# Loading adjacency chunks in transfers of 16 partitions instead of 8

## The chip, the cores and the metric

The kernel runs on one core of a Trainium2 chip. The metric is the device time of one execution in microseconds; lower is better. A separate execution is recorded by the hardware profiler, and all rows shown here come from that one.

## What is computed

Two graph layers over 4096 nodes with 128 features, each with a normalization ahead of it and a residual sum behind it. The adjacency is a 4096 x 4096 matrix of f32, 64 MiB, so reading it and keeping it in another order are the bulk of the traffic.

```python
h = relu(layernorm(x))
# layer 0
z = leaky_relu(lap_mul(adj, h) @ W1 + b1, 0.1)     # lap_mul(A, x) = d * (A @ (d * x)), d = 1/sqrt(row sums of A)
S = exp(-sqrt(pairwise squared distances of z) / 2), only the 4 largest of each row kept
x = x + lap_mul(S + adj, h) @ W2 + b2
# layer 1
h = relu(layernorm(x))
x = x + h @ W_self.T + (adj @ h) @ W_neigh.T + b
```

## The kernel before

The first stage reads the adjacency from HBM. A chunk is 2 MB: all 128 partitions, 16 rows of 256 columns each, so a partition gets 16 pieces of 1 KB that lie 64 matrix rows apart in HBM. There are eight groups g of four chunks c (`part_a`, in order of g and c), and then twelve chunks that are read a second time (`part_b`, groups from the last to the first): 44 chunks, 92.3 MB. They go into `araw`, which has four slots of one chunk; in `part_b` three of them are used.

GpSimd issues all loads (`load_first`, L367). Ahead of a chunk it waits until the chunk that was in the slot has been read (`chunk_read`). A chunk is split by `load_chunk`. The 128 partitions are four quarters q of R = 32; the transfers first take the quarters 0 and 2 in turn, then 1 and 3 in turn. SPREAD says how many transfers a quarter is split into and how far apart the partitions of one transfer are:

```python
def load_chunk(gp, g, c, place):
    for quarter_pair in ((0, 2), (1, 3)):
        for first in range(SPREAD):
            for q in quarter_pair:
                gp.dma_start(araw[R * q + first:R * q + R:SPREAD, place],
                             adj_v[q, first:R:SPREAD, g // 2, g % 2, :, c]).then_inc(a_first_in[place], DMA)
```

Whoever reads a chunk waits until the semaphore of its slot says that all of its transfers have landed (`PER_LOAD = QD * SPREAD * DMA`). ScalarE or VectorE sums its rows (`row_sums`, L618; L869), VectorE transposes it in blocks of 32 x 32 into units of 1 MB (`unit`, L840), and TensorE multiplies the units with the scaled features (`first_unit`, L1145). SyncE stores each of the 64 units to HBM (`transposed`, `keep_unit`, L408) for the later stages, while the loads go on. So in the first stage 92 MB are read on the queue of GpSimd, q0 in the trace, and 67 MB written on the queue of SyncE, q1; ScalarE's small stores of `hw_scratch` are on q10.

Behind it come the search for the four nearest nodes of each node (from about 500 us on), then two passes over the stored units. In them, GpSimd gathers rows with indirect transfers (L511, L587). Between the stages x is loaded once more (`xs`, 64 transfers of 32 partitions in 512 B pieces, each in one quarter, L428), and `hw_scratch` is loaded back by four transfers of 32 partitions, one for each quarter in turn (L447).

Of the kernel before, what the change touches and what calls it, by code (L numbers as in the profile page):

```python
# [42 lines left out]
SLOTS = 4  # L43
TSLOTS = 4
TOPK = 4
SPREAD = 4
LN_EPS = 1e-5
DMA = 16

# [1 line left out]
def gnn_kernel(nc, x, adj, W1, b1, W2, b2, W, b, out):  # L51
# [16 lines left out]
    with ctx:  # L68
# [251 lines left out]
        F1 = list(reversed(range(GROUPS)))  # L320
        PER_LOAD = QD * SPREAD * DMA
        X_IN = QD * GROUPS * DMA
# [40 lines left out]
# [7 lines that stand above are left out]
# [996 lines left out]
```

## Time and profile before

| | us |
|---|---|
| median of 3 runs (1219.0 to 1224.53) | 1224.19 |
| the profiled execution, its own time | 1223.94 |
| its span, first to last instruction | 1222.1 |
| TensorE busy | 969.5 |
| VectorE busy | 797.8 |
| GpSimd busy | 722.6 |
| ScalarE busy | 544.3 |

The span is a little shorter than the time of the execution. An engine's busy time counts its computing and, on GpSimd, the issuing of transfers; matrix multiplies overlap, so a busy TensorE isn't one at its peak. In the views of transfers, a queue's share is the time that its packets took, as a share of all 16 DMA engines over the stretch; since packets can overlap, a little over 100% can come out.

### The profile page before, as it was taken

What the parts mean: (1) busy time and instruction counts of PE and PEld (TensorE: products, weight loads), DVE (VectorE), ACT (ScalarE), POOL (GpSimd) and SP (SyncE); (2) the same over time, 40 slices, a digit from 0 to 9 for tenths busy, and PEclk for the clock granted to TensorE, in tenths of its full rate; (3) what the DMA queues carried; (4) which work ended last, traced back from release to release, by engine and by line L of the source; (5) the groups of instructions that cost most, each with busy time, mean ns of one, the idle gap of its engine ahead of it and who ended that gap; (6) DMA issues with size and microseconds to landing.
All of it is one profiled execution on the core that took longest, in us unless ns stands there. A gap on an engine that the chain in (4) does not pass through costs nothing.

```text
span 1222.1 us, 12797 instructions
## 1 busy us (share of the span) xinstructions
PE 969.5 (79%) x3506; PEld 649.9 (53%) x3506; DVE 797.8 (65%) x824; ACT 544.3 (45%) x1090; POOL 722.6 (59%) x1105
## 2 busy tenths in 40 slices
PE   0145635757868877899999996499999998999998
PEld 0122322323334333577777775266666666888886
DVE  1644644446357735399999999736666556788885
ACT  2455342644603211455555554523334334567663
POOL 9999999998839782144444444488778872000000
PEclk9977668878979989899999999699999999899999
DMA  9999999999999997685333336698888887699993
GB/s 219 322 313 329 316 336 358 350 364 350 376 349 369 367 366 281 189 271 214 139 141 141 142 143 225 196 365 329 312 309 303 305 327 273 244 385 392 363 392 110
DMA packets 126984, 353.67 MB, mean 289 GB/s; under 512 B 43232, under 2 KB 68576, under 8 KB 102368
## 3 DMA queue, kind: packets, MB, share of 16 engines
q1 hardware_dynamic: 55264, 243.75, 52.2%
q0 software_dynamic: 62464, 105.28, 29.3%
q10 hardware_dynamic: 9216, 4.20, 1.2%
q8 instruction: 14, 0.23, 0.1%
q14 instruction: 26, 0.21, 0.1%
HBM read 245.83 MB, written 106.95 MB: 289 GB/s over the span
## 4 chain that ended last, share of the span: by engine, by line
PE 31%; POOL 14%; issue 10%; DVE 6%; DMA 4%; ACT 2%; POOLq 0%; DVEq 0%; ACTq 0%; SPq 0%
POOL zt_lo L587 11%; PE ps L1255 5%; PE ps L1256 5%; PE ps L1257 5%; PE ps L1234 4%; PE ps L1237 4%; PE ps L1235 4%; PE ps L1236 4%; DMA araw<-in_adj_dram 3%; POOL araw L367 1%; POOL t_st L511 1%; DVE m L977 1%; PE ps L1145 1%; DVE i L979 1%; ACT araw L713 1%
## 5 line engine op out<-in xcount | busy, mean ns | idle before, releaser
L367 POOL DMA_DIRECT2D araw<-in_adj_dram x704 | 413.8, 597 | 44.1 <-DVE tr L840 28.3
L1089 DVE TENSOR_TENSOR araw_r<-araw,tr_r 128x2048 fp32r<-128x2048 f32 x96 | 217.5, 2289 | 89.6 <-ACT tr_r L740 89.5
L740 ACT ACTIVATE tr_r<-araw 128x2048 fp32r<-128x2048 f32 x96 | 181.4, 1910 | 81.2 <-DMA araw<-transposed 34.5
L587 POOL DMA_INDIRECT zt_lo<-neighbour_table,idx_st x128 | 175.9, 1374 | 46.0 <-issue 39.4
L713 ACT ACTIVATE araw<-ps,nsq 128x1024 f32<-128x1024 f32 x128 | 142.9, 1117 | 113.1 <-PE ps L1237 94.7
L1145 PE MATMUL ps<-tr,ys 128*128 128x512 f32 x256 | 131.8, 666 | 28.8 <-DVE ys L847 21.6
L618 ACT ACTIVATE ps<-araw 128x256 f32<-128x256 f32 x304 | 111.5, 367 | 84.0 <-DMA araw<-in_adj_dram 81.6
L1264 PE MATMUL ps<-araw,ys 128*128 128x512 f32 x256 | 117.0, 600 | 17.6 <-DVE ys L1012 17.6
L840 DVE STREAM_TRANSPOSE tr<-araw 128x2048 f32<-128x2048 f32 x32 | 72.8, 2295 | 67.7 <-DMA araw<-in_adj_dram 60.6
L869 DVE TENSOR_REDUCE part<-araw 128x16 f32<-128x4096 f32 x13 | 57.4, 4416 | 90.3 <-DMA araw<-in_adj_dram 62.0
L1234 PE MATMUL ps<-sq_rows,pick 128*128 128x512 f32 x256 | 102.2, 399 | 16.7 <-ACT araw L713 7.4
L1255 PE MATMUL ps<-araw_r,zt_hi 128*128 128x512 f32 x256 | 103.0, 402 | 4.9 <-DVE araw_r L1089 4.9
L1145 PEld LDWEIGHTS ps<-tr,ys 128*128 128x128 f32 x256 | 53.3, 216 | 93.8 <-issue 65.7
L1256 PE MATMUL ps<-tr_r,sq_rows 128*128 128x512 f32 x256 | 101.5, 396 | 0.0
L1257 PE MATMUL ps<-tr_r,zt_hi 128*128 128x512 f32 x256 | 101.2, 395 | 0.0
L1235 PE MATMUL ps<-zt_lo,zs_hi 128*128 128x512 f32 x256 | 100.5, 393 | 0.0
L1236 PE MATMUL ps<-zt_hi,zs_lo 128*128 128x512 f32 x256 | 100.4, 392 | 0.0
L1237 PE MATMUL ps<-zt_hi,zs_hi 128*128 128x512 f32 x256 | 100.4, 392 | 0.0
L511 POOL DMA_INDIRECT t_st<-keys_scratch,block_row x64 | 66.6, 1041 | 30.7 <-issue 25.1
L1264 PEld LDWEIGHTS ps<-araw,ys 128*128 128x128 f32 x256 | 48.7, 193 | 67.1 <-issue 65.1
L1171 PE MATMUL ps<-part,fold 128*128 128x16 f32 x64 | 14.1, 360 | 82.2 <-DVE part L869 82.2
L977 DVE MAX8 m<-araw 128x8 f32<-128x4096 f32 x16 | 70.9, 4430 | 9.7 <-ACT araw L713 9.3
(155 smaller groups left out, 1562.6 us busy)
## 6 DMA issues: line engine op xcount, KB each, us to landing
araw<-transposed SPq DMA_DIRECT2D x128, 1024.0 KB, 6.3
araw<-in_adj_dram POOLq DMA_DIRECT2D x704, 128.0 KB, 10.1
transposed<-tr SPq DMA_DIRECT2D x32, 1024.0 KB, 8.3
keys_scratch<-araw SPq DMA_DIRECT2D x64, 512.0 KB, 4.3
transposed<-unit_zt_hi SPq DMA_DIRECT2D x8, 1024.0 KB, 8.2
transposed<-unit_zt_lo SPq DMA_DIRECT2D x8, 1024.0 KB, 8.3
transposed<-unit_sq_rows SPq DMA_DIRECT2D x8, 1024.0 KB, 8.8
transposed<-araw SPq DMA_DIRECT2D x8, 1024.0 KB, 8.2
```

Of the source, the lines that this page charges most:

```text
L367: gp.dma_start(araw[R * q + first:R * q + R:SPREAD, place], adj_v[q, first:R:SPREAD, g // 2, g % 2, :, c]).then_inc(a_first_in[place], DMA)
L587: gp.indirect_dma_start(out=gath[:, i, u, k, :], out_offset=None, in_=table, in_offset=bass.IndirectOffsetOnAxis(ap=idx_st[:, i, u * TOPK ...
L713: act.activation(keys[par][:, c * 1024:c * 1024 + 1024], ps[:, 2 * c:2 * c + 2].rearrange("p a b -> p (a b)"), ACT.Identity, bias=nsq[:, b ...
L740: act.activation(ring_hi[:, place % TSLOTS], ring[:, j], ACT.Copy).then_inc(hi_done, 1)
L1089: v.tensor_tensor(ring_lo[:, j], ring[:, j], ring_hi[:, place % TSLOTS].bitcast(F32), ALU.subtract).then_inc(lo_done, 1)
L1145: pe.matmul(acc[bank], ys[:, i * GROUPS + j], rhs[:, i], start=start and i == 0, stop=stop and i == U - 1)\
L1234: pe.matmul(ps[:, c], pick[:], sq, start=True, stop=False)
L1235: pe.matmul(ps[:, c], zs_hi[:, par], zl, start=False, stop=False)
L1255: pe.matmul(acc[bank], hi[:, t], t_lo, start=j == 0 and i == 0, stop=False)
L1256: pe.matmul(acc[bank], lo[:, t], t_hi, start=False, stop=False)
L1257: ins = pe.matmul(acc[bank], hi[:, t], t_hi, start=False, stop=j == GROUPS - 1 and i == U - 1)
L1264: ins = pe.matmul(acc[bank], ys[:, i * GROUPS + j], ring[:, j, i], start=j == 0 and i == 0, stop=j == GROUPS - 1 and i == U - 1)
```

## The change

The number of transfers for a quarter goes from four to two, and with it the distance of the partitions of one transfer from four to two. A transfer then has 16 partitions instead of 8 and 256 KB instead of 128 KB, and a chunk is loaded by eight transfers instead of sixteen. The order of the quarters stays: 0, 2, 0, 2, 1, 3, 1, 3 now. The semaphore of a slot counts half as far, since `PER_LOAD` follows from the constant. Nothing else changes.

```diff
@@ -43,7 +43,7 @@
 SLOTS = 4
 TSLOTS = 4
 TOPK = 4
-SPREAD = 4
+SPREAD = 2
 LN_EPS = 1e-5
 DMA = 16
```

The instructions that GpSimd issues in the first stage, before (-) and now (+); a row gives the line, the operation, what it writes and reads, and its shape (partitions x pieces x elements) and number:

```order
@@ -8,5 +8,5 @@
 L484 AFFINE_SELECT ident<-ident 128x128
 L488 AFFINE_SELECT fold<-fold 128x128 x4
-L367 DMA araw<-in_adj_dram 8x16x256 x704
+L367 DMA araw<-in_adj_dram 16x16x256 x352
 L529 MEMSET sq_rows 64x4096
 L498 COPY zs_hi<-zt_hi 128x128
```

All other engines have the same instructions in the same order; on GpSimd the loads keep their place and there are half as many.

## Rows read from the trace of the kernel before

**Rows 1.** The page: span, then busy tenths in 40 equal slices.

```profile
span 1222.1 us, 12797 instructions
...
PE   0145635757868877899999996499999998999998
...
DVE  1644644446357735399999999736666556788885
ACT  2455342644603211455555554523334334567663
POOL 9999999998839782144444444488778872000000
...
DMA  9999999999999997685333336698888887699993
```

**Rows 2.** Transfers by queue from 0 to 485 us: packets, MB, share.

```profile
DMA packets 75095, 162.72 MB, mean 336 GB/s; under 512 B 35872, under 2 KB 44576, under 8 KB 67104
...
q0 software_dynamic: 56320, 92.68, 64.3%
q1 hardware_dynamic: 14144, 67.70, 35.2%
q10 hardware_dynamic: 4608, 2.10, 1.5%
```

**Rows 3.** Timeline of GpSimd: start, duration, instruction, count, idle before and releaser.

```profile
3.81 272.79 POOL L367 DMA_DIRECT2D araw<-in_adj_dram  x464 [0.37 <-POOL fold L488]
280.38 18.80 POOL L367 DMA_DIRECT2D araw<-in_adj_dram  x32 [3.79 <-ACTq L622]
```

**Rows 4.** Transfers from 77 to 86 us; an issue's last number is us to landing.

```profile
q0 software_dynamic: 1597, 2.63, 105.6%
...
araw<-in_adj_dram POOLq DMA_DIRECT2D x16, 128.0 KB, 4.5
```

**Rows 5.** The same from 270 to 300 us.

```profile
DMA packets 4339, 10.65 MB, mean 355 GB/s; under 512 B 2298, under 2 KB 2298, under 8 KB 3788
...
araw<-in_adj_dram POOLq DMA_DIRECT2D x44, 128.0 KB, 23.1
```

**Rows 6.** Waits from 0 to 520 us: who for whom, total, times, longest.

```profile
ACT ps L618 <- DMA araw<-in_adj_dram: 81.6, 11, 18.9
DVE part L869 <- DMA araw<-in_adj_dram: 62.0, 9, 14.7
DVE tr L840 <- DMA araw<-in_adj_dram: 60.6, 8, 19.0
```

**Rows 7.** The chain that ended last, about the last chunk: start, us, what.

```profile
460.76 20.46 DMA araw<-in_adj_dram
481.24 2.32 DVE araw L840
483.61 7.35 PE ps L1145 x16
```

**Rows 8.** Busy time by stretch; the last three numbers are PEclk, DMA share, GB/s.

```profile
0.00:30.00 30.00, 0.00 (x0) 0.00 (x0) 5.42 (x8) 7.77 (x33) 27.85 (x54) 1.00 0.93 218
```

**Rows 9.** Transfers from 519 to 524 us, when hw_scratch is loaded back.

```profile
DMA packets 2013, 1.06 MB, mean 213 GB/s; under 512 B 48, under 2 KB 1997, under 8 KB 2013
...
q1 hardware_dynamic: 1981, 1.00, 113.6%
```

**Rows 10.** Transfers from 493 to 508 us, when x is loaded again.

```profile
q1 hardware_dynamic: 4273, 1.95, 45.5%
```

**Rows 11.** Groups of GpSimd's instructions: busy, mean ns, idle before.

```profile
L367 POOL DMA_DIRECT2D araw<-in_adj_dram x704 | 413.8, 597 | 44.1 <-DVE tr L840 28.3 <-ACTq L622 8.9 <-DVE araw L840 5.4
L587 POOL DMA_INDIRECT zt_lo<-neighbour_table,idx_st x128 | 175.9, 1374 | 46.0 <-issue 39.4 <-POOL idx_st L583 6.6
```

## The prediction

> **What bounds the kernel now.** I read the page first, for where the transfers sit. The DMA row of the forty slices is full from the start to about slice 15, so the transfers are busy all through the first stage, while TensorE, VectorE and ScalarE stay at half or below there; the page also gives the span, 1222.1 us [rows 1]. The profiled execution took 1223.94 us by its own time, 1.8 us more than its span and 0.25 us under the median of 1224.19, so a sum made against it can be set against the median.
>
> Then the DMA view of the stretch in which the chunks are loaded, 0 to 485 us. The shares of all queues add up to 101% of 16 engines: 64.3% for q0, which carries GpSimd's loads, 35.2% for q1 with SyncE's stores, 1.5% for q10 [rows 2]. Nothing is left over. In engine time the loads take 0.643 x 485 x 16 = 4990 us, which is 7.09 us for each of the 704 transfers, and the stores take 0.352 x 485 x 16 = 2731 us for 67.70 MB, or 5.29 us for 128 KB. So 128 KB of a load cost 1.80 us of engine time more than 128 KB of a store. The packets say where that may go: 56320 packets over 704 transfers are 80 each, and 92.68 MB over 704 are 131.6 KB; in packets of 4 KB the data make 32, so some 48 of the 80 are small ones. The count under 512 B bears that out: 704 x 48 = 33792 of the 35872 [rows 2].
>
> GpSimd looks like a second bound and is nearly one. It issues 464 transfers without a pause in 272.79 us, 588 ns each, so it offers 223 GB/s of loads until 277 us, and only then starts to wait for free slots [rows 3]. What tells the two bounds apart is how long after its issue a transfer lands: 4.5 us (median) from 77 to 86 us, 23.1 us from 270 to 300 us [rows 4, 5]. The queue becomes deep, so the DMA engines decide, and GpSimd's pace matters in the first 180 us at most. In the stretch from 77 to 86 us the loads are alone, the share is 105.6%, and still only 292 GB/s come in [rows 4]: two transfers (256 KB) each 0.90 us. That is the limit of loads of this shape.
>
> Last, who waits. ScalarE's row sums wait 81.6 us for chunks, VectorE's sums and transposes 62.0 and 60.6 us [rows 6]. The chain ends the stage in the same way: the last issue at 460.76 us, 20.46 us until it lands, then a transpose at 481.24 us and its matmuls [rows 7]. What the loads gain or lose goes straight to the end, since all later stages start from there.
>
> **The change.** It removes 704 transfers of 8 partitions and adds 352 of 16, each within one quarter of the partitions. Bytes, 1 KB pieces, their order within a partition, chunks and waits are the same; a chunk's semaphore reaches half the count with half the transfers. Three things may cost or give.
>
> *GpSimd's issue.* No row shows an issue of 16 partitions. The lower bound is 588 ns whatever its size, 207 us in all; the upper is proportional, 1.18 us, 414 us in all, as now. Neither is in the way of the engines. I take nothing for it. At best it fills the start: from 0 to 30 us the share is 93% [rows 8], worth 0.07 x 30 = 2 us.
>
> *The small packets.* If their number goes by the transfer, half of them go. The most this gives is 352 x 1.80 / 16 = 40 us, when all of what loads cost above stores is theirs; the least is nothing, when that excess comes from the 1 KB pieces, which stay.
>
> *Where the bytes land.* Today two transfers in a row go to quarters 0 and 2 (then 1 and 3), with 8 partitions each; tomorrow the same 256 KB go to a single quarter, the next 256 KB to the other. The trace has loads that stay within one quarter: the four of hw_scratch, 32 partitions each. From 519 to 524 us they fill the engines (share 113.6% for q1) and bring 213 GB/s in total; 1981 packets, nearly all of 512 B, take 1.136 x 5 x 16 = 90.9 us of engine time, 46 ns each [rows 9]. The same size of packet takes less in the reload of x, also 32 partitions of one quarter but issued so slowly that the share is 45.5%: 0.455 x 15 x 16 us / 4273 = 25.6 ns [rows 10]. So the piece size alone doesn't make 213; engines crowded onto one quarter do, or such pieces under full load. At 213 GB/s, 256 KB take 1.231 us on all engines; now they take 2 x 7.09 / 16 = 0.886 us. Upper bound: 352 x (1.231 - 0.886) = +121 us. The lower bound is no loss, with the small packets' gain in full: -40 us.
>
> The Trainium skill (SBUF — State Buffer, section on the DMA port swizzle) speaks against this change: a transfer to partitions 0 to 31 reaches only 8 of 16 ports, and it gives 189 GB/s at 1 MiB. By that figure the estimate would be 352 x (1.387 - 0.886) = +176 us; this trace's nearest row, 213 GB/s, agrees in kind and is milder. The same skill (DMA: Bandwidth & Descriptors, section on why a DMA increments its semaphore by 16) says that the number of engines is the largest divisor of the slowest dimension up to 16, so 8 now and 16 after; no row here splits a queue by engine.
>
> Between -40 and +121 I take the middle, +41 us. The reason: hw_scratch keeps to one quarter for 512 KB a time, while here the side changes every 16 KB per engine, and a queue up to 23 us deep lets engines drift apart, so that about half of the time two that would collide are on different quarters. Half at 1.231 us and half at (14.18 - 1.80) / 16 = 0.774 us is 1.002 us, against 0.886 us: 352 x 0.116 = +41 us. 1223.94 + 41 = 1265 us. Stores read SBUF while loads write it; I give them no part in it. Everything after 485 us is moved, not changed.
>
> **Rivals.** *Full collision.* All engines stay in step, every transfer goes at 213 GB/s: +121, 1345 us. For it: they start each transfer together. Against it: the store traffic takes a third of their time and pulls them apart. Chance 0.16.
>
> *Faster.* Changing sides so often hides the collisions and the small packets halve: -40, 1184 us; with a third of the packets' gain, 1211 us. For it: the x reload brings its packets into one quarter at 25.6 ns each, with no sign of crowding [rows 10], and 292 GB/s for loads alone is far under the 355 GB/s of the mixed stretch [rows 4, 5], so overhead of each transfer is a likely culprit. It decides when collisions cost under 0.11 us per 256 KB. The skill's DMA page (rules for kernel authors) would have many small transfers coalesced; that goes this way. Chance 0.28.
>
> *Nothing.* Collisions eat what the packets give, or neither is real: 1224 us within 6. Chance 0.10.
>
> *GpSimd becomes the bound.* If 16 partitions cost more than twice, as dear as the mean gather of 1374 ns [rows 11], 352 of them take 484 us; issue now ends at 461 us with its waits included, so the stage ends some 25 us later, 1250 us. It decides from 1.3 us per issue on (352 x 1.3 = 458). Against it: the gather fetches its addresses, these don't. Chance 0.06.
>
> **The numbers.** The forecast (partial collision, +10 to +90 us, 1234 to 1314) has 0.40. Within 0.5%, 6 us, is what a measurement of this kernel can't tell from no change. Slower: 0.40 + 0.16 + 0.06 = 0.62; same 0.10; faster 0.28. The range goes from 1188, near the full gain, to 1330, four fifths of the way from the middle to full collision; about 0.1 is left out on either side.
>
> **What would show it.** In the profile after: q0's packets per transfer (112 if the 48 small ones go by the transfer, 160 if they go with the bytes); q0's engine time over the first stage, 4990 us now; GB/s in a stretch with loads alone, 292 now, about 262 by my middle, 213 by full collision, near 340 by the faster rival; the issue's duration, which should lie between 0.59 and 1.18 us; landing times, deeper than now. VectorE's and ScalarE's waits for chunks should grow by about the 41 us, the stages after the load should keep their lengths. I'm wrong if loads alone run over 292 GB/s, or if the last chunk lands before 481 us.

## The result and the profile after

The changed kernel takes 1243.29 us (median of 4 runs, 1235.68 to 1250.01), the kernel before 1223.93 us on the same chip (4 runs, 1219.0 to 1224.53). The ratio is 1.0165, with a 95% interval of 1.01 to 1.0231: slower by some 20 us. The profiled execution has a span of 1248.2 us against 1222.1 us, 26.1 us more; it is the longest of the four, and the rows below account for these 26 us.

The page of the changed kernel, as in [rows 1]: the span, then the busy tenths in 40 equal slices.

```profile
span 1248.2 us, 12445 instructions
...
POOL 7236343343322432024444444558778874000000
```

The transfers by queue from 0 to 510 us, where the first stage now ends, and the issues of the loads (KB each, median us to landing); this answers to [rows 2].

```profile
DMA packets 46900, 162.05 MB, mean 318 GB/s; under 512 B 7712, under 2 KB 16416, under 8 KB 38944
...
q0 software_dynamic: 28160, 92.30, 65.5%
q1 hardware_dynamic: 14112, 67.44, 33.9%
...
araw<-in_adj_dram POOLq DMA_DIRECT2D x352, 256.0 KB, 25.0
```

The same bytes are moved, the engines are as full as before (101%), and it takes 25 us longer. 28160 packets are 80 for a transfer of 256 KB: 64 of data and 16 small ones. In the kernel before, the same 256 KB had 160 packets, 96 of them small. So the packets did what the prediction hoped for and more, and still the kernel lost.

GpSimd's timeline (start, duration, instruction, count, idle before and releaser), the answer to [rows 3].

```profile
3.76 18.05 POOL L367 DMA_DIRECT2D araw<-in_adj_dram  x32 [0.32 <-POOL fold L488]
25.40 4.44 POOL L367 DMA_DIRECT2D araw<-in_adj_dram  x8 [3.59 <-ACTq L622]
33.18 4.44 POOL L367 DMA_DIRECT2D araw<-in_adj_dram  x8 [3.34 <-DVE part L869]
```

32 issues take 18.05 us, 564 ns each, with twice the partitions of before: nearly a fixed cost, just under the lower of the two bounds. GpSimd fills the four slots at once and waits from then on.

Now the stretches. First loads alone, 181 to 193 us (packets, MB, share), the answer to [rows 4].

```profile
DMA packets 901, 2.89 MB, mean 241 GB/s; under 512 B 175, under 2 KB 199, under 8 KB 900
...
q0 software_dynamic: 876, 2.87, 102.4%
```

Then a stretch with stores, 241 to 254 us.

```profile
DMA packets 1308, 5.40 MB, mean 416 GB/s; under 512 B 195, under 2 KB 465, under 8 KB 866
...
q1 hardware_dynamic: 490, 3.62, 66.8%
q0 software_dynamic: 500, 1.64, 31.3%
```

And one with stores in the kernel before, 222 to 237 us.

```profile
DMA packets 1965, 6.08 MB, mean 405 GB/s; under 512 B 723, under 2 KB 1034, under 8 KB 1452
...
q1 hardware_dynamic: 574, 4.19, 67.6%
q0 software_dynamic: 1031, 1.72, 31.9%
```

Here is where the time went, and where some came back. Alone, the loads fell from 292 GB/s [rows 4] to 241 GB/s. Beside stores nothing was lost, 416 against 405 GB/s in total, and a load is even cheaper there: 0.313 x 13 x 16 us / 1.64 MB = 39.7 us of engine time per MB, where before it was 0.319 x 15 x 16 / 1.72 = 44.5.

The stretches are typical. Of the windows of 3 us between 60 and 450 us, those without stores have 289 GB/s in the mean before and 242 now (38 and 37 windows). Those that move 370 GB/s or more in total have 45.0 and 41.1 us of engine time per MB of loads (55 and 57 windows). Over the whole stage the loads take 0.655 x 510 x 16 = 5344 us of engine time against 4990 before; the 354 us more are 22 us of all 16 engines, most of the 25.

There is a second difference, at the start. GpSimd issues the loads of all four slots in 18 us, and x, which SyncE loads beside them, lands later. VectorE's first instruction of the normalization (start, duration, instruction, count, idle before and releaser), before and then now:

```profile
43.14 6.29 DVE L854 BATCH_NORM_STATS2 out_t<-xs 128x6 f32<-128x128 f32 x32 [7.73 <-DMA araw<-in_adj_dram]
57.64 6.29 DVE L854 BATCH_NORM_STATS2 out_t<-xs 128x6 f32<-128x128 f32 x32 [24.76 <-DMA xs<-in_x_dram]
```

It starts 14.5 us later. The DMA engines are full in that time too, so no transfer time is idle because of it, but the first stores, which are behind x on the same queue, come later. No run took this delay away alone; one with the same delay is faster than the kernel before (stores of 4 KB rows, below).

The chain at the last chunk (start, us, what), the answer to [rows 7].

```profile
478.26 28.88 DMA araw<-in_adj_dram
507.17 2.32 DVE araw L840
509.54 9.32 PE ps L1145 x16
```

The last chunk lands at 507.1 us, 25.9 us later than before. Of the 26.1 us of loss, 25.9 lie ahead of that point.

### The profile page after: what moved, and what is told of

The parts are those of the page before. It is cut to its first block, busy times and chain, and to the rows that moved or that the text cites. A ratio compares the mean times of both kernels' runs of the same rounds, so it can differ in the third digit from the quotient of the medians.

```text
span 1248.2 us, 12445 instructions
## 1 busy us (share of the span) xinstructions
PE 973.6 (78%) x3506; PEld 651.6 (52%) x3506; DVE 797.6 (64%) x824; ACT 543.9 (44%) x1090; POOL 501.0 (40%) x753
## 4 chain that ended last, share of the span: by engine, by line
PE 44%; DMA 24%; DVE 14%; issue 6%; POOL 5%; ACT 3%; SPq 2%; ACTq 0%; POOLq 0%; DVEq 0%
DMA araw<-in_adj_dram 20%; PE ps L1264 9%; PE ps L1255 7%; PE ps L1256 7%; PE ps L1257 7%; PE ps L1145 3%; POOL araw L367 3%; DVE m L977 3%; DVE bmax L964 2%; DVE i L979 2%; SPq L398 2%; DMA xs<-in_x_dram 2%; PE ps L1234 2%; PE ps L1237 2%; PE ps L1235 2%
## 5 line engine op out<-in xcount | busy, mean ns | idle before, releaser
L367 POOL DMA_DIRECT2D araw<-in_adj_dram x352 | 195.9, 564 | 279.5 <-ACTq L622 118.5
## 6 DMA issues: line engine op xcount, KB each, us to landing
transposed<-tr SPq DMA_DIRECT2D x32, 1024.0 KB, 10.1
```

The lines of the kernel that those rows point to most:

```text
L367: gp.dma_start(araw[R * q + first:R * q + R:SPREAD, place], adj_v[q, first:R:SPREAD, g // 2, g % 2, :, c]).then_inc(a_first_in[place], DMA)
```

## Experiments

All kernels were run beside the kernel before on the same chip; times are medians. The changed kernel was not run again there, so a difference to it goes by way of the ratios. "Loads alone" is read from a stretch of the trace in which q1 moves nothing or next to nothing. The rate depends a little on the stretch. The means of all windows of 3 us without stores between 60 and 450 us are, in the order of the runs below, 196, 195, 185, 219, 214 and 265 GB/s for the first six, and they tell the same story.

**The order of the quarters, with the old transfers.** Two transfers in a row now go to quarters 0 and 1, not 0 and 2.

```diff
-            for quarter_pair in ((0, 2), (1, 3)):
+            for quarter_pair in ((0, 1), (2, 3)):
```

> Transfers of 8 partitions, four apart, 704 of them, as in the kernel before; only the order of the quarters is 0, 1, 0, 1 and then 2, 3, 2, 3. Theory A (what matters is which partitions are written at the same time: two transfers in a row on quarters 0 and 1 crowd, on 0 and 2 they don't): loads alone fall from 291 to about 246 GB/s as in the changed kernel, the time is about 1243 us. Theory B (the wider transfer itself is slow, by its form, packets or HBM rows): nothing changes, 291 GB/s and 1224 us.

1349.33 us against 1223.15 us, ratio 1.101 (1.0948 to 1.1072). The trace from 212 to 224 us, loads alone:

```profile
DMA packets 1399, 2.30 MB, mean 192 GB/s; under 512 B 840, under 2 KB 840, under 8 KB 1399
...
q0 software_dynamic: 1399, 2.30, 105.9%
```

Nothing but an order was changed, and loads alone fall from 292 to 192 GB/s. Theory A holds and theory B falls; the effect is far larger than either expected, larger than in the changed kernel.

**The distance of the partitions, with the old transfers.** 8 partitions, two apart instead of four.

```diff
-                for first in range(SPREAD):
+                for first in (0, 1, 16, 17):
                     for q in quarter_pair:
-                        gp.dma_start(araw[R * q + first:R * q + R:SPREAD, place],
+                        gp.dma_start(araw[R * q + first:R * q + first + 15:2, place],
```

> Transfers of 8 partitions as before, in the old order of quarters 0, 2 and 1, 3, but the partitions of one transfer are two apart instead of four. Theory A (crowding): loads alone at about 246 GB/s and a time near 1243 us, though number, size and packets of the transfers are those of the kernel before. Theory B1 (16 partitions in one transfer are slow): 291 GB/s, 1224 us. Theory B2 (HBM rows 32 KB apart instead of 64 KB): 246 GB/s as under A; the run with the other order of quarters tells these apart.

1349.51 us, ratio 1.1008 (1.0948 to 1.1069): the same as the run with the other order, to 0.2 us. From 204 to 228 us, with stores of 2.10 MB at its start (q0 has 82.1% of the engines over the whole stretch):

```profile
DMA packets 2660, 6.02 MB, mean 251 GB/s; under 512 B 1452, under 2 KB 1452, under 8 KB 2402
...
q0 software_dynamic: 2370, 3.91, 82.1%
```

3.91 MB in 0.821 x 24 us are 198 GB/s, an estimate that takes in what landed beside the stores. The number and size of the transfers are those of before, and small packets are again three of five (1452 of 2370), so what is left is which partitions, and with them which HBM rows, are in flight together. The distance of the HBM rows within a transfer did change here, but not in the run before, which has the same loss; so it isn't needed to explain it. Each run also changes which pieces of HBM are read one after the other, in a different way each time; that the loss is the same to 0.2 us speaks for the partitions, but no run changed the partitions and left the HBM side alone. Together the two fit one picture, which is inferred from them: what the engines write at the same time must lie in different places. Quarters 0 and 1 share such places, and so do partitions two apart. The Trainium skill (SBUF — State Buffer, section on the DMA port swizzle) draws them: four neighbouring partitions share a port with the four that lie 32 further on. Both runs agree with that map.

**16 partitions side by side.** The changed kernel with the closest partitions.

```diff
-                for first in range(SPREAD):
+                for first in (0, 16):
                     for q in quarter_pair:
-                        gp.dma_start(araw[R * q + first:R * q + R:SPREAD, place],
+                        gp.dma_start(araw[R * q + first:R * q + first + 16, place],
```

> The 352 transfers of the changed kernel with the 16 partitions of one side by side instead of two apart. Theory A (crowding, and it gets worse the closer the partitions): loads alone at about half of 246, 120 to 130 GB/s; 92 MB then take over 700 us and the kernel 1450 to 1550 us. Theory B (form of the transfer alone): as the changed kernel, 1243 us. The Trainium skill (SBUF - State Buffer, DMA port swizzle) puts 4 neighbouring partitions on one port, by which this is the doubled dose.

1354.24 us (2 runs), ratio 1.1062 (1.0962 to 1.1162). From 203 to 218 us, loads alone:

```profile
DMA packets 732, 2.34 MB, mean 156 GB/s; under 512 B 141, under 2 KB 165, under 8 KB 732
...
q0 software_dynamic: 708, 2.32, 102.5%
```

The direction is that of theory A, the size isn't: 156 GB/s here and near 195 in other stretches of this run, not 120 to 130, and the kernel is 100 us better than expected. The simple count of the expectation, half the places and so half the rate, overstates it. Which engine writes where was not read from any trace.

**32 partitions in a transfer.** SPREAD = 1.

> Four transfers of 32 partitions for a chunk, one for each quarter. Theory A: as crowded as the changed kernel, loads alone near 240 GB/s, about 1243 us, in spite of half the transfers. Theory B1 (the more partitions in a transfer the slower): slower than the changed kernel, 1260 us or more. If small packets by the transfer mattered, it would be faster than the changed kernel by 5 to 10 us.

1273.43 us, ratio 1.0393 (1.0345 to 1.0441). From 240 to 252 us:

```profile
DMA packets 794, 2.72 MB, mean 227 GB/s; under 512 B 82, under 2 KB 139, under 8 KB 792
...
q0 software_dynamic: 734, 2.68, 101.2%
```

As theory B1 said and A didn't: slower than the changed kernel. But one more thing differs. The transfers of one quarter are twice as large, so the side changes half as often. The next run takes that alone.

**The side held for longer.** The changed kernel's transfers, in another order.

```diff
-            for quarter_pair in ((0, 2), (1, 3)):
-                for first in range(SPREAD):
-                    for q in quarter_pair:
+            for q in range(QD):
+                for first in range(SPREAD):
```

> The transfers of the changed kernel, 352 of 16 partitions two apart, but in the order of quarters 0, 0, 1, 1, 2, 2, 3, 3, so that the side (quarters 0 and 1, or 2 and 3) changes once in a chunk instead of at each transfer. Theory P (crowding is the same whatever the order; the changed kernel is faster than the crowded 8-partition runs, 240 against 190 GB/s for loads alone, since it has 16 small packets for 256 KB instead of 96): 240 GB/s and 1243 us still. Theory D (engines drift apart and so write different sides half of the time, which the prediction assumed): with the side held, down to about 190 to 213 GB/s and 1300 us or more.

1283.26 us, ratio 1.0482 (1.046 to 1.0504), 40 us slower than the changed kernel by order alone. From 240 to 250 us:

```profile
DMA packets 653, 2.13 MB, mean 213 GB/s; under 512 B 132, under 2 KB 132, under 8 KB 653
...
q0 software_dynamic: 653, 2.13, 103.5%
```

213 GB/s is the rate of the hw_scratch loads [rows 9]; held on one side, the loads are as slow as these when alone. Changing sides does help, as theory D has it, though the time, 1283 us, stays under its 1300. Theory P's other half may have its part too. This run and the one with quarters 0 and 1 in turn both keep a side for 1 MB; one has 16 small packets for 256 KB and 213 GB/s, the other 96 and 192 GB/s. That is 1.231 against 1.365 us for 256 KB, 0.13 us for 80 small packets, if all of the difference is theirs, which isn't shown (a transfer also has twice the partitions).

**The side changed more often.** The changed kernel with each transfer cut in half along its pieces.

```diff
+                    for m in (0, 8):
                         for q in quarter_pair:
-                            gp.dma_start(araw[R * q + first:R * q + R:SPREAD, place],
-                                         adj_v[q, first:R:SPREAD, g // 2, g % 2, :, c]).then_inc(a_first_in[place], DMA)
+                            gp.dma_start(araw[R * q + first:R * q + R:SPREAD, place, m:m + 8],
+                                         adj_v[q, first:R:SPREAD, g // 2, g % 2, m:m + 8, c]).then_inc(a_first_in[place], DMA)
```

> The changed kernel with each transfer cut into two of 128 KB (16 partitions, 8 of the 16 pieces each), 704 in all, the order of quarters still alternating. Small packets double, from 16 to 32 for 256 KB. Theory P: 80 small packets fewer saved 0.29 us for 256 KB, so 16 more cost about 0.06 us: 1.09 to 1.15 us, loads alone 228 GB/s, 5 to 12 us slower than the changed kernel. Theory D: sides change twice as often, so no slower or faster than the changed kernel.

1227.56 us, ratio 1.0006 (0.9972 to 1.0039): 16 us faster than the changed kernel, with twice its transfers and small packets, and level with the kernel before. From 212 to 224 us:

```profile
DMA packets 1147, 3.13 MB, mean 261 GB/s; under 512 B 382, under 2 KB 382, under 8 KB 1147
...
q0 software_dynamic: 1147, 3.13, 104.4%
```

So with 16 partitions in a transfer, loads alone give 213, 241 and 261 GB/s as the side changes after 1 MB, 256 KB and 128 KB. The run with 32 partitions, which holds a side for 512 KB, fits in between with 227. Engines that drifted apart freely would not care how long a side is held. What evens it out isn't shown, and theory P alone is out.

The rates can be compared; the 16 us of time can't be put down to the sides alone. An issue carries half the bytes here, so x lands sooner beside the loads, and the normalization starts at 38.77 us instead of 57.64. And where the run with a side held for longer changes nothing but the order, this one also halves the transfers.

**Stores of 4 KB rows, loads as before.** SyncE's stores of 1 MB in two halves.

```diff
-                sp.dma_start(at[g, j], flat(units_t[unit_place[n]])).then_inc(at_out[unit_place[n]], DMA)
+                for k in range(0, U * GI, 1024):
+                    sp.dma_start(at[g, j, :, k:k + 1024], flat(units_t[unit_place[n]])[:, k:k + 1024]).then_inc(at_out[unit_place[n]], DMA)
```

> The kernel before, with SyncE's stores of 1 MB cut into two of 128 partitions x 4 KB; loads untouched. Theory M (loads and stores together always run at 400 to 420 GB/s, loads alone at 291, and a queue's part goes by the size of its packets): the stores, now in packets of 4 KB instead of 8 KB, take less of the engines while they run, more of the loads lie beside stores, loads run alone for less time, and the kernel gets faster, by up to 40 us; GpSimd's issue, 223 GB/s, keeps it from more. Rival (parts don't go by packet size, total engine time is what counts): 1224 us within 5, or a few us slower by the extra stores.

1222.58 us, ratio 0.9977 (0.9955 to 0.9998): next to nothing, which as a number is the rival's. From 60 to 180 us the loads still land 6.7 us after their issue, so GpSimd is ahead by only some 11 transfers there.

```profile
araw<-in_adj_dram POOLq DMA_DIRECT2D x205, 128.0 KB, 6.7
```

Its issues of 588 ns set the pace there, which the expectation named as the limit. GpSimd's timeline is that of the kernel before [rows 3], 464 issues in 272.79 us without a pause. A chunk can't land before it is issued, so up to 277 us other rows of the stores could not bring the loads in at more than that pace. Why the rest of the stage gave no more isn't shown, and no run took the limit away with the old transfers.

**Stores of 4 KB rows, loads as changed.** The same edit on the changed kernel.

> The changed kernel with the same cut of the stores. Theory M: the loss of the changed kernel sits only in the time when loads run alone, 224 of the 450 us from 30 us on, and is hidden beside stores; with the stores spread over more time it shrinks. So this run gains more from the cut than the kernel before does: 1243 down to 1200 or less. Rival: crowding costs the same beside stores, and this run stays 20 us behind the kernel before with the same stores.

1205.93 us, ratio 0.9854 (0.9824 to 0.9883), close to the 1200 us or less of theory M and far from the rival's. The same cut of the stores is worth 37 us here and 2.5 us there, and with these stores the transfers of 16 partitions are 17 us faster than those of 8. From 200 to 216 us, beside stores:

```profile
DMA packets 1897, 6.54 MB, mean 409 GB/s; under 512 B 300, under 2 KB 300, under 8 KB 1897
...
q1 hardware_dynamic: 947, 3.42, 53.4%
q0 software_dynamic: 950, 3.12, 48.9%
```

The total is that of before, but the loads' part rose from 1.64 MB in 13 us (126 GB/s) to 3.12 MB in 16 us (195 GB/s). The engines now spend less of the stage with loads alone. By the DMA view's slices of 0.75 us between 30 and 480 us, those under 310 GB/s make 177 us in the kernel before, 223.5 us in the changed one, and 147.75 us here. They make 147.75 us in the run before this one as well, which gained 2.5 us; so less time with loads alone pays only where GpSimd can issue faster than they land. This run still has the late x of the changed kernel (normalization at 57.71 us), so that delay doesn't by itself make a kernel slower than the one before.

**Both cuts.** Loads in halves and stores of 4 KB rows.

> The changed kernel with both cuts: loads in 704 transfers of 16 partitions and 128 KB, sides alternating every 8 KB for an engine, and stores in two of 128 partitions x 4 KB. Theory S (the shorter a side is held the less the crowding costs, and crowding costs only while loads run alone) together with M (4 KB stores leave less time with loads alone): faster than either alone (1227.6 and 1205.9 us), 1190 to 1203 us. Rival G (704 issues of GpSimd at 0.52 us or more offer at most some 250 GB/s and set the pace as in the kernel before): 1206 us or slower, with landing times that stay short in the first 200 us.

1204.51 us, ratio 0.9846 (0.9804 to 0.9887). The two gains don't add: once few loads run alone, what speeds up loads alone is worth 1 us, within the noise. The time lies between the 1190 to 1203 us of the first theory and the 1206 us of rival G, and the sign that G named is missing: landing times are 14.8 us in the median of 60 to 120 us, so GpSimd hardly sets the pace.

**Stores of 2 KB rows, loads as changed.** The loop over k in steps of 512.

> The changed kernel with each store cut into four of 128 partitions x 2 KB. Theory M (a queue's part goes by the size of its packets): with 2 KB packets loads beside stores rise from 193 GB/s (4 KB) towards 250, loads alone nearly vanish, and the time is at or below 1206 us; but more small packets and issues take some of it back. Rival (the 4 KB cut helped for another reason, its shorter transfers): the loads' rate beside stores stays at about 193 GB/s.

1212.03 us (8 runs), ratio 0.9904 (0.9869 to 0.9939), 6 us slower than with 4 KB. From 200 to 300 us:

```profile
DMA packets 15635, 36.28 MB, mean 363 GB/s; under 512 B 2351, under 2 KB 3887, under 8 KB 15630
...
q0 software_dynamic: 6948, 22.78, 65.8%
q1 hardware_dynamic: 6954, 12.67, 35.0%
```

The loads' rate did what theory M said: 22.78 MB in 100 us are 228 GB/s, well over 193, and their part of the engines is 65.8%. So the rival is out. The two queues send as many packets as each other, 6948 and 6954, with the loads' still of 3.3 KB in the mean and the stores' now of 1.8 KB. It was so with 4 KB rows (950 and 947) and in the changed kernel (500 and 490), though not in the kernel before (1031 and 574). As if the queues took turns, a queue then gets engines by the size of its packets.

The time is what theory M had wrong. The total falls to 363 GB/s here, from 409 with 4 KB rows. And the stores fall behind: up to 330 us the loads are ahead, 72.6 MB against 67.2 with 4 KB rows, and then VectorE and ScalarE wait for stores, which they do in neither kernel and in no run with 4 KB rows (who for whom, total, times, longest, 0 to 520 us):

```profile
ACT zt_hi L686 <- DMA transposed<-unit_sq_rows: 29.0, 1, 29.0
DVE tr L841 <- DMA transposed<-tr: 13.7, 3, 6.2
DVE unit_zt_lo L841 <- DMA transposed<-unit_zt_lo: 11.9, 2, 6.2
```

A transpose that waits for its unit to be stored frees no slot. From 330 to 390 us only 5.06 MB of loads come in, and the lead is gone: 90.0 against 90.8 MB at 450 us.

## Why the prediction was right in direction and wrong in size

**What bounds the stage, and that its loss reaches the end:** right. Shares of 101% in both kernels, and 25.9 us at the last chunk against 26.1 us of span. One sign named for it failed: VectorE's and ScalarE's waits for chunks [rows 6] were to grow by about 41 us, and they add up to 200.6 us where they were 204.2. The wait moved elsewhere, 24.8 us of it to VectorE's wait for x at the start.

**GpSimd's issue at nothing:** right in that it bounds nothing now; 564 ns, just under the lower bound of 588. What I made too little of is that the old transfers held the start back to 223 GB/s. That pace hides in the kernel before, and it came to matter only with other stores. What its end is worth in the changed kernel wasn't measured apart from the rest.

**The upper bound, +121 us for full collision at 213 GB/s:** right as a rate, wrong as a time. The changed kernel's transfers with the side held do run at 213 GB/s alone, but they cost 58 us, not 121, since that rate holds only without stores. The crowded runs of 8 partitions lost 126 us, at 192 GB/s alone.

**The step that failed** is the one sentence "Stores read SBUF while loads write it; I give them no part in it", and with it the term of +0.116 us on each of the 352 transfers. Over the whole stage that term measured 354 us of engine time / 16 / 352 = +0.063 us, half of it. The split shows why. Alone, the collision costs more than the middle I took: 0.2621 MB at 241 instead of 292 GB/s is 1.088 against 0.898 us, +0.19 us. Beside stores it costs nothing, and a gain is left over that fits the small packets: 39.7 instead of 44.5 us of engine time per MB, which is (10.41 - 11.66) / 16 = -0.08 us for 256 KB. A rough estimate puts the two together, taking every slice under 310 GB/s as loads alone and the costs from two stretches: the slices hold 223.5 us x 247.6 GB/s = 55 MB of the 92 MB, so 211 transfers ran alone and 141 beside stores: 211 x 0.19 - 141 x 0.08 = 40 - 11 = +29 us, against 26 in the profiled execution and 20 in the medians. That it comes so close is in part luck, as the limit of 310 is a choice. The mean over all transfers is what a share over the whole stage gives, and it mixed two costs that the change moves in opposite directions. Since [rows 5] already showed 355 GB/s beside stores and [rows 4] 292 without, the split was there to be made.

**The reason given for the middle,** engines that drift apart in a deep queue, is at best half right, and that the middle of two bounds gave the right sign is in part luck. Alternating sides does help, by 40 us against holding one. But how much depends on how many bytes a side is held, which drift over a deep queue would not explain. What smooths it wasn't measured.

**The rivals.** Faster by small packets: loads beside stores did get cheaper, which fits their gain, but no run changed their number alone, and it is outweighed while loads run alone. With stores of 4 KB rows that rival's direction wins, 1206 against 1223 us. Full collision is the rate of loads alone with the side held; no run has it for every transfer. GpSimd as the bound is out. Of the signs named, 262 GB/s for loads alone by the middle came out as 241, between the middle and full collision, and q0's packets as 80 for a transfer, fewer than either of the two counts that I gave, 112 and 160. Landing times did get deeper, 25.0 us in the median against 10.1.

## What to carry to other kernels

When a queue's transfers get wider, look at which partitions are written at the same time, not only at their number and size: with the very same transfers, the order of the quarters was worth 126 us here. Split a stage into stretches with and without the other queue before costing a change of a transfer, since a loss that is full alone can be nothing beside other traffic. And the rows of the competing stores decide how much of the load lies beside them: with rows of 4 KB instead of 8, the changed loads came to 1206 us, 1.5% under the kernel that they had made 1.65% slower. There is an end to it: with rows of 2 KB the loads got still more, the stores fell behind, and the time rose to 1212 us.

## What the runs showed of the hardware that was not expected

- An issue of GpSimd grows little with the 1 KB pieces: 532 ns for 128 pieces and 564 ns for 256 (16 partitions), 650 ns for 512 (32 partitions). With 8 partitions, 128 pieces take 588 ns.
- A transfer of 8 partitions has 48 small packets, one of 16 has only 16. This was counted from the views, and why it is so wasn't settled.
- Loads together with stores of 8 or 4 KB rows move 405 to 416 GB/s whether the loads crowd or not, loads alone between 156 and 292 GB/s. With stores of 2 KB rows the two together move 363 GB/s.
- Transfers of 16 neighbouring partitions get more than half of the rate of 16 partitions two apart: 156 to 195 GB/s against 213 to 241.
- Cutting the stores' rows from 8 to 4 to 2 KB moves the changed loads' part of the engines beside them from 31.3% to 48.9% to 65.8%, while the two queues send equal numbers of packets each time.
